# Moving the attention products to the end of a head pair in a transformer block kernel on one core

## The reference

```python
shift = silu(t) @ W_ada.T + b_ada
h = _ln(x, ln1_g, ln1_b) + shift
qkv = (h @ Wqkv.T).reshape(b, n, 3, H, HD)
q = _ln(qkv[:, :, 0].transpose(0, 2, 1, 3), qn_g, qn_b)
k = _ln(qkv[:, :, 1].transpose(0, 2, 1, 3), kn_g, kn_b)
v = qkv[:, :, 2].transpose(0, 2, 1, 3)
scores = einsum('bhnd,bhmd->bhnm', q, k) / sqrt(HD)
attn = softmax(scores, axis=-1)
o = einsum('bhnm,bhmd->bhnd', attn, v)
x = x + o.transpose(0, 2, 1, 3).reshape(b, n, H * HD) @ Wout.T
gate = softmax(tok @ Wgate.T, axis=-1)          # tok = x as (4096, 256)
vals, idx = top_k(gate.T, k_cap)                # k_cap = 512 tokens for each expert
g = _ln(tok[idx_flat], mlp_g, mlp_b)
y = gelu(g @ fc1.T + b1) @ fc2.T + b2           # per expert
tok = tok.at[idx_flat].add(y * w)
```

## Time and profile before

| | |
|---|---|
| time, three runs | 1157.24 us median, 1156.55 to 1157.64 |
| profiled execution | 1159.4 us, span 1157.6 us |
| granted TensorE clock, mean | 0.989 |
| busy PE, DVE, ACT, POOL (share of the span) | 95%, 78%, 63%, 52% |
| 110 to 830 us: busy PE, DVE, ACT, POOL | 709.3, 582.1, 519.1, 429.4 of 720 us |

### The profile page before, as it was taken

How to read it: one execution, slowest core, us unless ns; L and a number is a source line. 1 busy time by engine, 2 the same in 40 slices (tenths; PEclk the granted TensorE clock), 3 DMA queues, 4 the chain that set the end, 5 groups by cost and what they waited for, 6 DMA issues and landing times.

```text
span 1157.6 us, 24504 instructions
## 1 busy us (share of the span) xinstructions
PE 1101.2 (95%) x8046; PEld 860.9 (74%) x8052; DVE 899.9 (78%) x1693; ACT 731.6 (63%) x1991; POOL 607.3 (52%) x529
## 2 busy tenths in 40 slices
PE   8899999999999999999999999999988779999996
PEld 6667777777777777777777777777765248889985
DVE  6897888878887878788787878787776867777773
ACT  5667777776767677777777676777773214455441
POOL 2556555666666556656565665656562023554332
PEclk9899999999999999999999999999999998999999
DMA  5000000000000000000000000000002404554422
GB/s 184 17 10 19 20 20 19 18 18 18 18 18 20 27 25 18 18 18 18 18 18 18 18 18 18 30 15 20 10 19 84 132 18 132 168 134 119 109 29 28
DMA packets 31776, 48.62 MB, mean 42 GB/s; under 512 B 7921, under 2 KB 28529, under 8 KB 30449
## 3 DMA queue, kind: packets, MB, share of 16 engines
q1 hardware_dynamic: 25584, 39.49, 10.5%
q0 software_dynamic: 6144, 8.52, 4.0%
HBM read 35.29 MB, written 12.71 MB: 41 GB/s over the span
## 4 chain that ended last, share of the span: by engine, by line
issue 31%; PE 31%; POOL 21%; DVE 8%; ACT 6%; POOLq 1%; DMA 1%; SPq 0%; ACTq 0%; DVEq 0%
POOL qk_lo L1076 9%; POOL prob L1059 5%; PE ch L508 5%; PE ch L510 4%; PE ch L509 4%; POOL qn L965 3%; PE av L1689 3%; DVE m L1470 2%; PE sc L1590 2%; ACT prob L1170 2%; ACT raw L1125 1%; PE sc L508 1%; PE sc L510 1%; PE sc L509 1%; PE pq L1643 1%
## 5 line engine op out<-in xcount | busy, mean ns | idle before, releaser
L1059 POOL TENSOR_TENSOR prob<-prob,inverse 128x1024 f32<-128x1024 f32 x127 | 241.1, 1899 | 265.4 <-DVE inverse L1398 265.4
L1170 ACT ACTIVATE prob<-sc,m 128x256 f32<-128x256 f32 x512 | 235.9, 475 | 121.3 <-DVE m L1470 118.2
L1470 DVE TENSOR_REDUCE m<-sc 128x4 f32<-128x1024 f32 x127 | 155.4, 1224 | 69.9 <-PE sc L1590 69.7
L1419 DVE COPY probT<-mx 128x1024 f32<-128x1024 f32 (+1 forms) x128 | 155.2, 1212 | 59.2 <-PE mx L1634 58.1
L1076 POOL TENSOR_TENSOR qk_lo<-qkT,qk_hi 128x512 fp32r<-128x512 f32 x128 | 171.5, 1340 | 26.0 <-ACT qk_hi L1152 24.5
L508 PE MATMUL ch<-w_hi,hT_lo 128*128 128x512 f32 x384 | 170.1, 443 | 2.6 <-DVE hT_lo L1332 2.2
L509 PE MATMUL ch<-w_lo,hT_hi 128*128 128x512 f32 x384 | 152.3, 397 | 0.0
L510 PE MATMUL ch<-w_hi,hT_hi 128*128 128x512 f32 x384 | 152.0, 396 | 0.0
L1689 PE MATMUL av<-probT,V 128*64 128x256 f32 x1024 | 139.6, 394 | 8.3 <-DVE probT L1419 3.8
L1634 PE MATMUL mx<-con,prob 128*128 128x128 f32 x1024 | 134.5, 274 | 9.1 <-POOL prob L1059 7.8
L1634 PEld LDWEIGHTS mx<-con,prob 128*128 128x128 f32 x1024 | 116.0, 140 | 29.0 <-POOL prob L1059 11.7
(11 more groups left out here) (222 smaller groups left out, 2686.9 us busy)
## 6 DMA issues: line engine op xcount, KB each, us to landing
fcw<-experts SPq DMA_DIRECT2D x8, 2048.0 KB, 9.0
x_sb<-x SPq DMA_DIRECT2D x16, 256.0 KB, 2.7
xr_sb<-x SPq DMA_DIRECT2D x16, 256.0 KB, 2.8
out<-tok SPq DMA_DIRECT2D x16, 256.0 KB, 2.2
rows_dram<-xh SPq DMA_DIRECT2D x16, 256.0 KB, 2.2
prob<-w_qk SPq DMA_DIRECT2D x2, 512.0 KB, 6.5
qn<-w_qk SPq DMA_DIRECT2D x2, 512.0 KB, 7.2
V<-w_vT SPq DMA_DIRECT2D x2, 512.0 KB, 7.3
```

The costliest lines, as they stand in the source:

```text
L1059: nc.gpsimd.tensor_tensor(pr, pr, r, ALU.mult).then_inc(normalised, 1)
L1170: ins = nc.scalar.activation(prob[hp % 2][:, g * N:(g + 1) * N], sc[:, g * N:(g + 1) * N], ACT.Exp, bias=m[hp % 2][:, g:g + 1], scale=-1.0 ...
L1419: nc.vector.tensor_copy(probT[:, 0:half], mx[:, 0:half]).then_inc(probT_ready, 1)
L1470: nc.vector.tensor_reduce(m[hp % 2][:, :], sc[:, :].rearrange("p (g n) -> p g n", n=N), AX.X, ALU.min).then_inc(max_ready, 1)
```

## The change

On PE the attention product moves from the place between the first filling and the scores to the end of the pair, after the second filling, where the transposes of the next pair follow it. In pair 6 the gate products move behind the second part of the projection, next to the attention product. The input transposes move from the end of pair 1 to pair 2, behind the transposes of q and k. ACT and DVE follow: `o_hi` (`attended_high`) now stands between the second and the third exponential of the pair; in pairs 1 and 5 the first V chunk is read behind `o_hi` and the second V chunk behind the fourth exponential; DVE's `o_lo` (`attended_low`) becomes the last thing of a pair. The table of counts lists the gate behind the projection. The new order holds where `under` or `filled` is true, which is every pair of batches 0 to 14 and pairs 0 to 2 of batch 15; the other pairs of batch 15 and the drain keep theirs. No instruction is added or removed.

```diff
--- before.py
+++ after.py
@@ -89,9 +89,10 @@
 
     for b in range(-1, B + 1):
         cur, nxt, prv = 0 <= b < B, b + 1 < B, 1 <= b <= B
+        for hp, pos, name, who in sorted(batch_slots(b), key=lambda s: (s[0], 3 if s[2] == "gate" else s[1])):
+            hit("slot", b, (hp, pos))
         for hp, pos, name, who in batch_slots(b):
             key = (hp, pos)
-            hit("slot", b, key)
             hit(who, b, key)
             if name == "gate":
                 slots[-1] = (b, (6, 0), who, key)
@@ -1172,11 +1173,22 @@
                     if first > 0:
                         ins.then_inc(prob_ready, 1)
 
+                def attended_high(hp, u):
+
+                    need(attended, u - 1)
+                    if hp == 2 and prv:
+                        need(slot_filled, through("slot", b - 1, (6, 2)))
+                    if hp == 6 and prv:
+                        need(slot_filled, through("slot", b, (2, 0)))
+                    nc.scalar.activation(o_hi[:, (hp - 2) % UNITS, :], av[:, 0:N], ACT.Copy).then_inc(o_hi_ready, 1)
+
                 for hp in range(UNITS):
                     u = b * UNITS + hp
                     par = (hp + 1) % 2
                     ahead = (cur and nxt) or (cur and hp < UNITS - 1) or (nxt and hp == UNITS - 1)
                     live = (hp, 0) in CHUNKS and (cur if hp < 2 else nxt)
+                    behind = (cur and hp > 1) or (hp < 2 and prv)
+                    under = cur and (nxt or hp < 3)
                     if ahead:
 
                         need(qk_transposed, u + 2)
@@ -1215,14 +1227,9 @@
                         other_transposed(u)
                     if tail and hp == UNITS - 1:
                         exponentials(u, hp, 0)
-                    if (cur and hp > 1) or (hp < 2 and prv):
-                        need(attended, u - 1)
-                        if hp == 2 and prv:
-                            need(slot_filled, through("slot", b - 1, (6, 2)))
-                        if hp == 6 and prv:
-                            need(slot_filled, through("slot", b, (2, 0)))
-                        nc.scalar.activation(o_hi[:, (hp - 2) % UNITS, :], av[:, 0:N], ACT.Copy).then_inc(o_hi_ready, 1)
-                    if live and values:
+                    if behind and not under:
+                        attended_high(hp, u)
+                    if live and values and not under:
                         chunk(b, hp, 0)
                     if ahead and not (tail and hp > 1):
                         split_high(u, par)
@@ -1230,12 +1237,18 @@
                         power_guess(b, 0)
                     if hp == 5 and nxt and not entry:
                         power_guess(b, 4)
-                    if live and values:
+                    if live and values and not under:
                         chunk(b, hp, 1)
                     if cur and not (tail and hp == UNITS - 1):
                         exponentials(u, hp, 0)
+                    if behind and under:
+                        attended_high(hp, u)
+                    if live and values and under:
+                        chunk(b, hp, 0)
                     if cur:
                         exponentials(u, hp, TT)
+                    if live and values and under:
+                        chunk(b, hp, 1)
                     if tail and hp == 5:
                         power_guess(b, 4)
 
@@ -1403,8 +1416,17 @@
             def batch(b, cur, nxt, prv):
                 last_entry = isinstance(b, int) and b == B
                 entry = isinstance(b, int) and b < 0
+
+                def attended_low(hp, u):
+
+                    need(o_hi_ready, u - 1)
+                    pair = (hp - 2) % UNITS
+                    nc.vector.tensor_tensor(o_lo[:, pair, :], av[:, 0:N], o_hi[:, pair, :].bitcast(F32), ALU.subtract).then_inc(o_split, 1)
+
                 for hp in range(UNITS):
                     u = b * UNITS + hp
+                    behind = (cur and hp > 1) or (hp < 2 and prv)
+                    under = cur and (nxt or hp < 3)
                     if entry and hp == 2:
                         silu_of_condition()
                         low_parts(0, 0)
@@ -1472,11 +1494,8 @@
                         variances(b, hp)
                     if hp == 2 and nxt and not entry:
                         split_rows(b)
-                    if (cur and hp > 1) or (hp < 2 and prv):
-
-                        need(o_hi_ready, u - 1)
-                        pair = (hp - 2) % UNITS
-                        nc.vector.tensor_tensor(o_lo[:, pair, :], av[:, 0:N], o_hi[:, pair, :].bitcast(F32), ALU.subtract).then_inc(o_split, 1)
+                    if behind and not under:
+                        attended_low(hp, u)
                     if hp in (0, 3, 4, 7) and (cur if hp < 2 else nxt):
                         head_sums(b, hp, 0)
                     if hp == 3 and has_second(b):
@@ -1607,6 +1628,24 @@
                         ins = nc.tensor.transpose(bank[:, c * N + t * P:c * N + (t + 1) * P], rows[:, t, c * P:(c + 1) * P], ident)
                 ins.then_inc(slot_filled, 1)
 
+            def attend(b, hp, u, drain):
+
+                need(probT_ready, u - 1)
+                if drain:
+                    need(probT_other_ready, hp + 1)
+                need(o_split, u - 2)
+                i = (hp - 2) % GU
+                gpar = ((hp - 2) // GU) % 2
+                if i == 0:
+
+                    need(act_read, through("act", b, (1, 1)) if hp == 6 else through("act", b, (0, 0)) - 1)
+                for jt in range(TT):
+                    for hh in range(2):
+                        at = (hh * TT + jt) * N
+                        ins = nc.tensor.matmul(av[hh * HD:(hh + 1) * HD, 0:N], V[gpar][:, jt, i * P + hh * HD:i * P + (hh + 1) * HD],
+                                               probT[:, at:at + N], start=(jt == 0), stop=(jt == TT - 1))
+                ins.then_inc(attended, 1)
+
             def batch(b, cur, nxt, prv):
                 drain = isinstance(b, int) and b == B
                 for hp in range(UNITS):
@@ -1642,6 +1681,10 @@
                         for c, at in ((0, 0), (2, 1), (1, 2), (3, 3)):
                             ins = nc.tensor.transpose(pq[:, at * P:(at + 1) * P], qn[gpar][:, c, i * P:(i + 1) * P], ident)
                         ins.then_inc(qk_transposed, 1)
+                    if hp == 2 and nxt and cur:
+                        bank = take_bank(b, (1, 2))
+                        need(xh_ready, b + 2)
+                        transposed(bank, xh)
                     if live:
                         chunk(b, hp, 0)
                     if hp == 6 and prv:
@@ -1672,31 +1715,22 @@
                     filled = nxt or hp < 3
                     if cur and not filled:
                         scores(u, hp % 2)
-                    if behind:
-
-                        need(probT_ready, u - 1)
-                        if drain:
-                            need(probT_other_ready, hp + 1)
-                        need(o_split, u - 2)
-                        i = (hp - 2) % GU
-                        gpar = ((hp - 2) // GU) % 2
-                        if i == 0:
-
-                            need(act_read, through("act", b, (1, 1)) if hp == 6 else through("act", b, (0, 0)) - 1)
-                        for jt in range(TT):
-                            for hh in range(2):
-                                at = (hh * TT + jt) * N
-                                ins = nc.tensor.matmul(av[hh * HD:(hh + 1) * HD, 0:N], V[gpar][:, jt, i * P + hh * HD:i * P + (hh + 1) * HD],
-                                                       probT[:, at:at + N], start=(jt == 0), stop=(jt == TT - 1))
-                        ins.then_inc(attended, 1)
+                    if behind and not filled:
+                        attend(b, hp, u, drain)
                     if cur and filled:
                         scores(u, hp % 2)
                     if live:
                         chunk(b, hp, 1)
-                    if hp == 1 and nxt:
+                    if hp == 1 and nxt and not cur:
                         bank = take_bank(b, (1, 2))
                         need(xh_ready, b + 2)
                         transposed(bank, xh)
+                    if hp == 2 and prv:
+                        need(o_split, u - 2)
+                        project(second, (7,) if drain else (6, 7), True)
+                    if hp == 6 and cur:
+                        need(o_split, u - 2)
+                        project(first, (2, 3), True)
                     if hp == 6 and prv:
                         bank = ch[slot_bank(b, (6, 1))]
                         need(act_read, through("act", b, (6, 0)))
@@ -1705,12 +1739,8 @@
                                 ins = nc.tensor.matmul(bank[:, t * E:(t + 1) * E], tokT[:, c, t * P:(t + 1) * P], wg_sb[:, c, :],
                                                        start=(c == 0), stop=(c == DC - 1))
```

(8 more changed lines are left out.)

## The result

The changed kernel takes 1175.21 us (median of 4 runs, 1174.64 to 1175.9) against 1156.89 us (4 runs, 1156.08 to 1157.64) for the kernel before on the same chip: ratio 1.0159, 95% interval 1.0143 to 1.0175, so 18.3 us or 1.6% slower. The forecast was 1188 with a range of 1171 to 1206. The profiled execution took 1175.04 us, its span 1173.2, at a mean granted clock of 0.995 (0.989 before).

The account below looks back on a forecast made before the run. PE bounds the kernel, its records covering 709 of 720 us. Edges +1.2 and waits +1.0 make 2.2 us in each of batches 1 to 14, 31 us: 1190 profiled, 1188 us median, 2.7% slower; range 1171 to 1206.

Parts of the forecast that it names:

- The edges: PE's changes of array shape: four per pair instead of three, 0.70 us, 0.15 more, in 121 pairs 18.5 us.
- The edge between f32 transposes and fp32r products costs nothing: On PE: changing number format is free; only changes between full array, half columns and half rows cost.
- The old waits: PE's waits in the kernel before, 1.8 us a batch: 0.5 in pair 7, 1.3 in pairs 2 to 5.
- part 2: Waits that go: the attention product's on the probT copy; scores 1 us earlier bring probabilities earlier against the next transposes.
- The bank wait of pair 2: PE's projection (2,0) wants its bank at 8.2 us, freed by ACT's second V read at 8.8: wait 0.75.
- The bank wait of pair 6: Token transposes wait 0.3 us on the first V, projection (6,2) 1.0 on the second: 1.3, bounds 0.75 and 1.7.
- I put `m` at T + 4.9 to 6.1: DVE's minimum, timed from pair start T, 3.31 us of work from the probT copy; it makes pair 6's third exponential late.
- the floor: Least bank wait, 0.75 us, following from the order of ACT's six instructions behind the attention product.
- Pair 7: PE waits 0.7 us: 0.6 at the second chunk for DVE's projection sum, 0.1 for inverse before pair 0.
- Batch 0: No (2,0) or (6,0) user there, so its waits fall by about as much as its edges add.
- the case's own range: 1174 to 1203 us, from bounds of the entry (-8, +7) and of the bank waits (-11, +8).
- only the edges cost: Rival, 11%: ACT gets V chunks read in time, old waits stay at 1.8 us; time 1157 + 18.5 = 1176.

Follow-up runs that it names:

- e1: Changed kernel with ACT's second V chunk read ahead of the third and fourth exponential in pairs 1 and 5; 1164.23 us, ratio 1.0059 to the kernel before.
- e4: Kernel before with half of the scores ahead of the attention product and half behind, one more change of shape; 1191.63 us, ratio 1.0292.
- e10: e1 plus e8's wait of POOL for DVE's xh; 1159.06 us, ratio 1.0007 to the kernel before.
- e3: Kernel before with the scores ahead of the attention product in every pair, ACT and DVE unchanged; 1169.3 us, ratio 1.0099.
- e5: e3 with ACT's qk_hi and deviation guess ahead of o_hi, second V between the exponentials; 1139.01 us, ratio 0.9843 to the kernel before.
- e8: Kernel before with POOL made to wait for DVE's xh ahead of qk_lo in pair 6; 1150.37 us, ratio 0.9938.

## Why the prediction was right, and where it was off

**The edges (18.5 us): right.** I forecast 6.39 us for a pair, with the four edges at 0.20, 0.20, 0.14 and 0.16; measured 6.39, with 0.196, 0.20, 0.144 and 0.158. "The edge between f32 transposes and fp32r products costs nothing" also held: 0.00 to 0.005 us at every such change after. It doesn't hold for the gates, f32 products of 8 columns: 0.08 us behind them in before, which the new order saves, so that e1's pair 6 is 7.67 and not my 7.77. e4 prices one more change at 0.19 by another route.

The Trainium skill, TensorEngine Tiling (Array Packing), Key Properties, says that a change of tiling mode drains the engine; that each of the four edges above has a price agrees with it, though no row here shows the draining itself.

**The old waits (1.8 a batch) go: right in part 2, and more so than I had it.** None is left; in e10, without the bank waits, a batch is 53.28 for the wait-free 53.0, and 0.4 of waiting is back in pair 3 alone.

**The bank wait of pair 2 (0.75): right,** 7.63 for 6.87, with the releaser that I named, and the second V read by T + 8.8 in pair 1 as forecast; e1 removes it by moving that one instruction. (8.8 + 0.1 - 8.2 is 0.7; the sum in the prediction was rounded up.)

**The bank wait of pair 6: 1.3 forecast, 0.73 measured (8.50 for 7.77; 0.83 against e1's 7.67).** The step that failed is "I put `m` at T + 4.9 to 6.1". It began at 559.95, T + 4.4. DVE and POOL after:

```profile
556.64 1.22 DVE L1441 COPY probT<-mx 128x1024 f32<-128x1024 f32 x1
...
558.65 0.69 DVE L1373 TENSOR_REDUCE ssum<-sq 128x8 f32<-128x512 f32 x1 [0.27 <-ACT sq L1128]
559.26 0.69 DVE L1386 TENSOR_SCALAR var<-mv 128x4 f32<-128x4 f32 x1
...
559.95 1.21 DVE L1492 TENSOR_REDUCE m<-sc 128x4 f32<-128x1024 f32 x1
```
```profile
558.03 1.90 POOL L1060 TENSOR_TENSOR prob<-prob,inverse 128x1024 f32<-128x1024 f32 x1 [2.88 <-DVE inverse L1411]
```

From the copy to `m` there are 3.31 us, exactly as in the earlier trace rows: `var` is shorter than in the pair that I had read (0.69 for 1.06 us), but DVE now waits for ACT's `sq` ahead of it. What is earlier is the copy itself, T + 1.13 where pair 5 of before has T + 1.74 (medians of 12 batches). My T + 4.9 took a start near the old one. Why DVE reaches the copy earlier is not shown. `var`, with its four columns, ends as POOL's normalisation ends (559.95 and 559.93), of which more below. With `m` earlier, only the order of ACT's six instructions sets the wait, and that is the floor which I had as my lower bound:

```profile
562.11 0.38 ACT L1183 ACTIVATE o_hi<-av 128x256 fp32r<-128x256 f32 x1
562.37 0.61 ACT L1131 ACTIVATE V<-ch 128x512 f32<-128x512 f32 x1
562.85 0.49 ACT L1171 ACTIVATE prob<-sc,m 128x256 f32<-128x256 f32 x1
...
563.75 0.63 ACT L1131 ACTIVATE V<-ch 128x512 f32<-128x512 f32 x1
```

The second V is read by 564.38, 2.48 behind the pair's start at 561.90; I had forecast 2.4 for pair 2 and 3.0 here. The token transposes, for which I had 0.3 of waiting, don't wait: the first V is read by 562.98 and they start at 563.26.

**Pair 7: 0.7 forecast, none measured.** I took 2.50 for the two `xh` from the earlier trace rows as if it were their own length. After:

```profile
569.75 1.62 DVE L1350 TENSOR_SCALAR xh<-x_sb,mv,rstd 128x256 f32<-128x256 f32 x2
...
573.21 0.67 DVE L1396 TENSOR_TENSOR xr_sb<-xr_sb,ch 128x512 f32<-128x512 f32 x1
...
574.45 0.16 DVE L1411 RECIPROCAL inverse<-row_sum 128x4 f32<-128x4 f32 x1
```

In the changed kernel POOL and DVE meet differently, and only one of the two `xh` runs beside POOL. The sum is read by T + 3.5, not 4.3. When e1 removes pair 6's wait, both meet it again (2.36) and 0.5 appears. e10 takes that 0.5 away by keeping POOL off one `xh`, so the length of `xh` is the cause. My terms were not independent: this wait appears only where the bank waits are gone.

**Batch 0 (about 0): wrong, 2.8 in the two profiled executions and some 4.7 at one clock.** "Its waits fall by about as much as its edges add" was not read from any row. DVE is the late engine there; a later o_hi makes it idle, which is a part of the loss.

In sum, from my 1190 for the profiled execution to the measured 1175: the edges as forecast; waits 1.5 a batch where I had 2.8, 18 us less over 14 batches; batch 0 +2.8, of which 0.9 are its six edges; the end of the kernel 1.0 less. So the time lies in the range partly by luck: two waits were put too high, and a term that I had put at nothing took part of that back. The lower end of "the case's own range", 1174, is also not the sum of its bounds, 1188 - 8 - 11 = 1169. The rival "only the edges cost" has the right number (1176), but not its mechanism: it left the old waits in place and denied the bank waits, and both are shown otherwise. Two misses cancelled in it.

## What to carry to other kernels

When an engine's list is reordered, price the edges by distances between starts, then look one engine further: what stands in the queue behind the instruction that reads the moved result? Here that decided between 1% slower (e3) and 1.6% faster (e5), with the same order on PE. A duration read next to another engine's work is a duration in that company; before it goes into a sum, find the same instruction with the other engine idle.

## What the runs showed of the hardware that was not expected

A DVE tensor_scalar on operands in SBUF beside a POOL instruction doesn't slow down in proportion; it ends just behind POOL's instruction, `xh` 0.15 us behind it in every batch of after and e8 (13 each). `xh` from `x_sb` is on average 1.29 us in before (26 of 26 beside POOL); in after 13 are free of POOL at 0.402 and 13 beside it at 1.31; in e8 13 at 0.40 and 13 at 1.21; `xh` from `tok`, the same operation and shape, never meets POOL and takes 0.40 us. e8 shows the cause by taking it away.

The Trainium skill, SBUF — State Buffer, SBUF: two separate sides, says that the two engines share a pair of ports under an exclusive lock, kept for a whole instruction by the one that starts first, and that the other "fully blocks"; for DVE it names instructions in a two-port mode or with two inputs in SBUF. These numbers agree, but no profile here tells in which mode `xh` runs, and the first `xh` starts 0.01 to 0.02 us ahead of POOL's `qn` and is still the one held up.

POOL is held up by DVE too. In before its `qk_lo` takes 1.27 to 1.33 us, but 1.73 in pair 2, where DVE's `hT_lo` began 0.83 ahead of it, and `qn` takes 1.23 for 1.04 where DVE's `hT_hi` began 0.43 ahead:

```profile
530.89 0.75 DVE L1331 CAST hT_hi<-hT 128x512 fp32r<-128x512 f32 x1
531.67 1.42 DVE L1332 TENSOR_TENSOR hT_lo<-hT,hT_hi 128x512 fp32r<-128x512 f32 x1
```
```profile
531.31 1.23 POOL L965 TENSOR_TENSOR qn<-raw,rstd 128x512 f32<-128x512 f32 x1
532.50 1.73 POOL L1076 TENSOR_TENSOR qk_lo<-qkT,qk_hi 128x512 fp32r<-128x512 f32 x1
```

No run takes this away, as e8 does for `xh`. POOL's wait of 0.64 us in e8 costs nothing that shows; I put that down to POOL being busy only about half of the time.
